# A state-space layer with its feed-forward on one core: the later sequences' first chunks of x turned by VectorE and memory, and the new state one projection tile later

## The reference, cut to what matters

```python
proj = input_states @ in_proj_w.T                 # gate, x, B, C, dt
xBC = silu(depthwise_conv(xBC) + conv_b)          # 4 taps
dt = softplus(dt + dt_bias); cum = cumsum(dt * A) # within a chunk
scores = (C @ B^T) * exp(cum_i - cum_j) * mask * dt_j
y_intra = scores @ x
state   = cdec * state + (dt * dlast * x)^T @ B   # carried over chunks
y_inter = (C * exp(cum)) @ state_before
g = (y_intra + y_inter + D * x) * silu(gate)
x = x + (g * rsqrt(mean(g^2) + eps)) * norm_w @ out_w.T
x = x + ffn(layernorm(x))                         # SwiGLU with low-rank terms
```

## Time and profile before

| | us |
|---|---|
| median of 3 runs | 1725.38 |
| lowest and highest | 1725.22, 1727.03 |
| time of the profiled execution | 1728.03 |
| its span, first to last instruction | 1726.2 |
| mean granted TensorE clock, share of full | 0.997 |

### The profile page before, as it was taken

How to read it: one execution, slowest core, us unless ns; L and a number is a source line. 1 busy time by engine, 2 the same in 40 slices (tenths; PEclk the granted TensorE clock), 3 DMA queues, 4 the chain that set the end, 5 groups by cost and what they waited for, 6 DMA issues and landing times.

```text
span 1726.2 us, 27380 instructions
## 1 busy us (share of the span) xinstructions
PE 1697.8 (98%) x9541; PEld 1406.2 (81%) x9541; DVE 1302.7 (75%) x2202; ACT 1194.5 (69%) x2232; POOL 1228.3 (71%) x1058
## 2 busy tenths in 40 slices
PE   8889999999999999999999999999999999999999
PEld 7768888888888888888888888888888888787887
DVE  8888688968797879778886879687977799663323
ACT  6857777776877777767877777778777777663411
POOL 5567778777787878777878778777877787774510
PEclk9999999999999999999999999999999999999999
DMA  5564636555655455554745565555555573554201
GB/s 185 159 177 132 171 115 207 154 157 159 198 157 146 142 158 190 152 166 133 201 128 170 149 199 160 156 158 176 154 152 151 149 212 114 156 148 135 83 12 49
DMA packets 156617, 261.96 MB, mean 152 GB/s; under 512 B 28097, under 2 KB 57409, under 8 KB 156481
## 3 DMA queue, kind: packets, MB, share of 16 engines
q1 hardware_dynamic: 156480, 260.21, 51.8%
HBM read 230.25 MB, written 29.89 MB: 151 GB/s over the span
## 4 chain that ended last, share of the span: by engine, by line
PE 89%; DVE 5%; POOL 2%; DMA 2%; issue 1%; ACT 1%; SPq 0%; DVEq 0%; POOLq 0%; ACTq 0%
PE bank L1813 18%; PE bank L1815 17%; PE bank L1814 17%; PE bank L1891 7%; PE bank L1942 6%; PE bank L1935 6%; PE bank L1952 6%; PE bank L1906 4%; DVE ow_l L1458 2%; PE bank L2197 1%; PE bank L2196 1%; PE bank L2198 1%; PE bank L1968 1%; DVE bcT L1452 1%; PE bank L1875 1%
## 5 line engine op out<-in xcount | busy, mean ns | idle before, releaser
L763 POOL TENSOR_TENSOR w_l<-w_raw,w_h 128x512 fp32r<-128x512 f32 x288 | 398.0, 1384 | 267.3 <-ACT w_h L967 267.1
L1813 PE MATMUL bank<-x_h,w_h 128*128 128x512 f32 (+1 forms) x1328 | 527.7, 397 | 10.2 <-DVE bcT L1452 5.9
L1815 PE MATMUL bank<-x_h,w_l 128*128 128x512 f32 (+1 forms) x1328 | 519.4, 391 | 0.0
L1814 PE MATMUL bank<-x_l,w_h 128*128 128x512 f32 (+1 forms) x1328 | 518.7, 391 | 0.0
L1020 ACT ACTIVATE decay<-decay,cols 128x128 f32<-128x128 f32 x1024 | 318.3, 390 | 9.8 <-POOL decay L769 8.1
L1452 DVE SCALAR_TENSOR_TENSOR x_ch<-bank,par,x_ch 128x511 f32<-128x511 f32 (+2 forms) x384 | 286.3, 746 | 34.1 <-ACT x_ch L985 25.0
L1813 PEld LDWEIGHTS bank<-x_h,w_h 128*128 128x128 f32 (+1 forms) x1328 | 249.8, 188 | 64.6 <-issue 12.3
L1815 PEld LDWEIGHTS bank<-x_h,w_l 128*128 128x128 f32 (+1 forms) x1328 | 249.5, 188 | 54.2
L1814 PEld LDWEIGHTS bank<-x_l,w_h 128*128 128x128 f32 (+1 forms) x1328 | 250.0, 188 | 50.6
L769 POOL TENSOR_SCALAR_AFFINE_SELECT decay<-decay 128x512 f32<-128x512 f32 x256 | 200.3, 799 | 73.0 <-DMA decay<-cum_scratch 72.0
L1506 DVE TENSOR_TENSOR decay<-decay,bank 128x512 f32<-128x512 f32 x256 | 171.0, 682 | 82.6 <-ACT decay L1020 82.6
(11 more groups left out here) (164 smaller groups left out, 2793.5 us busy)
## 6 DMA issues: line engine op xcount, KB each, us to landing
w_raw<-in_wp SPq DMA_DIRECT2D x288, 256.0 KB, 3.5
decay<-cum_scratch SPq DMA_DIRECT2D x256, 256.0 KB, 4.7
x_rows<-xt_scratch SPq DMA_DIRECT2D x48, 512.0 KB, 3.3
ec<-ecum_scratch SPq DMA_DIRECT2D x96, 256.0 KB, 7.0
ow_raw<-in_ow SPq DMA_DIRECT2D x64, 256.0 KB, 5.4
xt_scratch<-xw_sq SPq DMA_DIRECT2D x128, 128.0 KB, 3.0
w_raw<-in_w SPq DMA_DIRECT2D x48, 256.0 KB, 2.7
xt_scratch<-ec_sq SPq DMA_DIRECT2D x64, 128.0 KB, 2.4
```

The costliest lines, as they stand in the source:

```text
L763: pool.tensor_tensor(w_l[:, s, :], w_raw[:, s, :], w_h[:, s, :].bitcast(F32), ALU.subtract).then_inc(wl_ready, 1)
L1813: pe.matmul(dst, wh, xh, start=(opens and k == 0), stop=False)
L1814: pe.matmul(dst, wh, xl, start=False, stop=False)
L1815: last = pe.matmul(dst, wl, xh, start=False, stop=(k == len(terms) - 1 and not more))
```

## The change

1. `on_pe(K)` is true for K = 0, 1 and 2 alone. Chunks 1 and 2 of the first group now go by TensorE as chunk 0 does, and the first chunks of all later sequences (K = 4, 8, ..., 60) go by DVE and memory.
2. There are four scratch areas and four semaphores in memory, one for each c, where there were two. The turned x of a chunk with c = 0 lies in `gT_sq` (the bytes of `gT_l`), that with c = 2 in `xh_sq` (the bytes of `xw_h`). The fetched rows for c = 0 go to `xw`.
3. In a slot with c = 3, DVE turns the next chunk right behind `add_skip`, ahead of `mean_square` and `gated`; SP stores it, stores the chunk two further, and then waits for the first store to land and fetches it. DVE's `scale_x` stands behind the first quarter's `scores` in place of ahead of `accumulate`. POOL's `gT_low` there waits for the store, since it writes where `gT_sq` lay.
4. In a slot with c = 0 (not K = 0), TensorE computes the first projection tile ahead of `new_state`, the second behind it, and then `match` and `across`. DVE does `mean_square` and `gated` ahead of `add_state`.
5. At the start, DVE's `turn_x(0, 1)` and its store are gone, and POOL's `gT_low` no longer waits for `xdt_ready` where the next chunk goes by TensorE. In the first three chunks `new_state` waits for `xdt_ready`, since it writes the banks that `scale_x` reads.

The diff, cut to its core:

```diff
-            return ec_sq if k % SC == 1 else xw_sq
+            return (gT_sq, ec_sq, xh_sq, xw_sq)[k % SC]
+        def rows_at(k):
+            return xw if k % SC == 0 else x_rows
+        def on_pe(K):
+            return K < SC - 1
+        def moved_no(K):
+            return K - SC + 2
@@ SP, fetch_x
-                sp.wait_ge(x_stored[K % 2], stored_no(K))
-                if some(K - 1):
+                if on_pe(K):
+                    return
+                sp.wait_ge(x_stored[K % SC], stored_no(K))
+                if k % SC > 0:
                     sp.wait_ge(out_done, 2 * (K - 1))
-                sp.dma_start(x_rows[:, :], xt_dram[K % 2]).then_inc(x_fetched, 16)
+                sp.dma_start(rows_at(k)[:, :], xt_dram[K % SC]).then_inc(x_fetched, 16)
@@ SP, body
-                    if c == 1 or first:
+                    if c == 1:
                         store_x(g, k + 2)
                     if c == SC - 1:
+                        store_x(gn, kn)
                         store_x(gn, kn + 2)
+                        fetch_x(gn, kn)
@@ POOL, gT_low
                 pool.wait_ge(gTh_ready, K + 1)
-                if c < SC - 1:
+                if c == SC - 1 and K < GROUPS * CHUNKS - 1:
+                    pool.wait_ge(x_stored[0], stored_no(K + 1))
+                elif K < GROUPS * CHUNKS - 1 and not on_pe(K + 1):
                     pool.wait_ge(xdt_ready, K + 2)
@@ ACT, xw_high
+                if k % SC == 0 and some(K):
+                    act.wait_ge(x_stored[2], stored_no(K + 2))
@@ DVE, body
                     add_skip(g, k)
+                    if c == SC - 1:
+                        turn_x(gn, kn)
                     if first:
                         ...
+                    elif c == 0:
+                        mean_square(*before)
+                        gated(g, k)
+                        add_state(g, k)
                     else:
                         add_state(g, k)
                         mean_square(*before)
                         gated(g, k)
...
+                    if c == SC - 1:
+                        accumulate(*before)
+                        turn_x(gn, kn + 1)
+                        scores(gn, kn, 0)
                     scale_x(gn, kn)
@@ TensorE, body
+                    late_state = c == 0 and not first
+                    if late_state:
+                        projects(tiles[:1])
                     new_state(g, k)
                     if first:
                         projects(tiles[3:4])
-                    if not first:
+                    if late_state:
+                        projects(tiles[1:2])
+                    elif not first:
                         ...
                     if last and c == SC - 1:
                         match(gn, kn)
                         projects(tiles[1:-1])
-                        turn_x(gn, kn)
                     else:
-                        if c == SC - 1:
+                        if on_pe(gn * CHUNKS + kn):
                             turn_x(gn, kn)
                         match(gn, kn)
```

More of the change, by code:

```diff
@@ L180, in build @@
         xdt = sc("xdt", [P, GCH])
+        xh_sq = under("xh_sq", [P, QUADS, CT, SQ])
         xw_h = sc("xw_h", [P, GCH], F32R)
@@ L189, in build @@
         x_rows = under("x_rows", [P, GCH])
+        gT_sq = under("gT_sq", [P, QUADS, CT, SQ])
         gT_l = sc("gT_l", [P, CT, P], F32R)
@@ L334, in build @@
         x_turned = sem("x_turned")
-        x_stored = [sem(f"x_stored{n}") for n in range(2)]
+        x_stored = [sem(f"x_stored{n}") for n in range(SC)]
         x_fetched = sem("x_fetched")
@@ L695, in body @@
                             load_decay(gn, kn, q)
-                    if c == 0:
+                    if c == 0 and some(K):
                         sp.wait_ge(x_stored[1], stored_no(K + 1))
@@ L784, in weigh_x @@
                 if c == 2:
[L785 to L789, removed]
+                    pool.wait_ge(x_stored[SC - 1], stored_no(K + 1))
                 pool.tensor_tensor(per_head(xw[:, :]), per_head(xdt[:, :]), spread(cols[:, b, ELAST, c, :], HDIM),
@@ L1490, in turn_x @@
                 dve.wait_ge(silu_done, conv_no(2 * g + b, CONV_TILES))
-                if c == 1 and some(K - 1):
+                if c == 0:
+                    dve.wait_ge(out_done, 2 * (K - 1))
+                if c == 1:
                     dve.wait_ge(z_scaled, n_across(g, k))
                 if c == 2:
-                    dve.wait_ge(st_done, n_state(g, k - 2) if some(K - 2) else 1)
+                    dve.wait_ge(st_done, n_state(g, k - 2))
                 if c == SC - 1:
@@ L1758, in body @@
                             ow_low(g, j)
+                    if c == SC - 1:
+                        accumulate(*before)
+                        turn_x(gn, kn + 1)
+                        scores(gn, kn, 0)
                     scale_x(gn, kn)
-                    if not first:
+                    if not first and c < SC - 1:
                         accumulate(*before)
-                    if c == SC - 1:
-                        turn_x(gn, kn + 1)
                     if k == 0:
@@ L1771, in body @@
                     taps_of(tiles[1:2])
+                    if k == 0 and not first:
+                        fade(gn, kn)
                     if k > 0:
                         scale_across(gn, kn)
-                        scores(gn, kn, 0)
+                        if c < SC - 1:
+                            scores(gn, kn, 0)
                         scores(gn, kn, 1)
@@ L2161, in body @@
                     if not first:
-                        projects(tiles[1:3])
+                        projects(tiles[2 if c == 0 else 1:3])
                     out_half(g, k, 0)
```

42 lines of the change are left out of this document (19 added, 23 removed).

## The result

| | before | changed |
|---|---|---|
| median, us | 1725.77 (4 runs) | 1801.85 (4 runs) |
| profiled execution, its span | 1728.03, 1726.2 | 1801.73, 1799.9 |
| mean granted clock | 0.997 | 0.979 |

The ratio is 1.043, 95% interval 1.0418 to 1.0443. The forecast was 1750 (1730 to 1775): the sign was right and the place too, the size was not. The spans differ by 73.7 us. Compared by the starts of TensorE's 64 `inside` blocks in both timelines, they fall so: -10.2 up to slot K = 4; +80.0 in the 14 slots K = 4 to 56 that follow a border, 4.8 to 7.0 in each; -0.4 in the 14 slots ahead of those borders; +5.1 in slot K = 59; -0.8 behind. All other slots agree within 0.1.

A forecast was written before the change was run, and what follows sets the result against it. TensorE's list was taken to bound the kernel. Borders +21, last border +2, slots k = 0 +6, start -8 and clock +3 gave +24 on the median 1725.38: 1749.4, rounded to 1750 us, range 1730 to 1775.

The forecast's parts named there:

- What bounds the kernel: Whole kernel: TensorE, busy 1697.8 of 1726.2 us; only its work removed or its waits change the time.
- The chain at the border: Store, fetch, `scale_x`, POOL, ACT, `scores` at 14 borders: TensorE stands 2.1 us in `inside`, net +1.5 each, +21.
- lands 3.3 later: Border chain: the fetch of x, issued at T + 5.1, lands 3.3 us later, at T + 8.4.
- By the Trainium skill: Border DMAs estimated at 2.3 us a store, 3.2 the fetch; each border 0.8 cheaper, still a loss.
- Transposes taken off: TensorE at the borders: 15 turns of 0.63 us go, -9.5; two come at K = 1, 2, +1.3.
- The step on POOL: Border chain: `weigh_x` takes 1.92 us, to T + 11.7; `gT_low` ahead, starting with the landed store, is long done.
- The clock: Behind the stands of 2.1 us at the borders: half clock at 2 of 14, +3 (0 to 24).
- The rival: Same stands, but half clock for 3.4 us behind most borders, 24 in place of 3: about 1771; chance 0.15.
- Slots k = 0: State one tile later: 0.9 us more wait for DVE's taps in each of 7 groups, +6 (3 to 9).
- The start: First chunks: the fetch chain behind TensorE's 6.58 us wait and the half clock go, -8 (-11 to -4).
- The last border: Last group's border: DVE's `norm_apply` behind `scale_x` comes 3.3 us late for TensorE, net +2 (0 to 4).
- SP's list: Rival: SP's wait for the landed store delays the loads behind it, 2 us more a border, 1778; chance 0.05.

The follow-up runs named there:

- e2_state: The kernel before with the new order of the slots c = 0 alone; 1727.99 us, ratio 1.0008.
- e5_delay: The kernel before with mutually waiting ACT copies ahead of the fourth exponentials, a different count at each of 14 borders, new tile placed last; 1775.64 us, ratio 1.0280.
- e12_fetch: The changed kernel with the store of `xh_sq` put behind the fetch of x in place of ahead of it; 1777.99 us, ratio 1.0278.
- e3_xwh: The changed kernel with ACT's `xw_high` behind the last exponentials in slots with c = 3; 1776.9 us, ratio 1.0287.
- e4_delay: The kernel before with 8 to 30 one-column ACT copies ahead of the last exponentials, another number at each of 14 borders; 1746.65 us, ratio 1.0112.
- e6_order: The changed kernel with `xw_high` behind the last exponentials, POOL's sums ahead of `weigh_x` and DVE's four `scores` ahead of `scale_x`, where c = 3; 1781.4 us, ratio 1.0308.

## Why the prediction was wrong

- **What bounds the kernel**: right. Only TensorE's list counted, and all 80 us lie where five lists meet at the border.
- **The chain at the border**: right in every link and order. It was short by 1.85 at its end: 0.4 at the store's landing, 1.5 in the fetch, nothing behind it. The step that failed first is the fetch that "lands 3.3 later": that term took the median of fetches of other slots and measured 4.8 to `scale_x`. "Two other stores are still under way, which may stretch it" had the cause, and was given no number. The stretch of the changed kernel above shows DMA engines 0.92 busy during the fetch; where a fetch of before runs I had not read it. It is 0.72 (366.6 to 369.9, the same columns):

```profile
366.60:369.90 3.30, 3.30 (x40) 2.91 (x37) 2.17 (x8) 2.10 (x4) 3.30 (x3) 1.00 0.72 235
```

  The fourth quarter came 3.3 late in place of 2.1, and with 0.5 to 0.7 more behind it (drains behind ACT's `xw_high`, and the restart) it was 3.8 a border: 54 us where the sum had 29.
- **By the Trainium skill**, "DMA: Bandwidth & Descriptors", the anatomy of one DMA: the estimate from its fixed part and its rate was 3.2 for the fetch. The rows have 4.6 here and 3.8 without the store ahead: the fit has no term for what is queued ahead, which here cost 0.8.
- **Transposes taken off**: the 0.63 at 14 borders was not gained. It was to be 8.8 us and is 0.4, since TensorE now waits for POOL's `gT_l` ahead of `inside` (the row at 364.09: 0.43, and a slower start behind it), which waits for the landed store. The step on POOL named that wait ("starts with the landed store") and looked only at what POOL did next, not at TensorE, which wants `gT_l` at T + 7.6.
- **The clock**: "2 borders of 14: +3" failed; it was 14 of 14 and about 24 us in the tile behind the stand alone (4.58 in the mean, 2.85 for the same order in e2_state), some 2 more where half clock lasted 6.8 us. I had set 2.1 between the rows at 1.53 and 2.48 and taken the cheap side. In this place e5_delay had full clock up to 1.72 and half clock from 1.97, e12_fetch half clock at 12 of 14 stands of 2.08 to 3.07; in e3_xwh, with stands of 1.44 to 2.11 ahead of `square_total`, it came 10 times of 14. A fourth quarter that is 3.3 late shows as 3.0 of idle time in the row, so the forecast's 2.1 would be some 1.8 there (an estimate from these two), between e5_delay's 1.72 and 1.97: the longer chain carried the stands past what had left full clock there. The rival had this mechanism, 1771 with a chance of 0.15; the longer stands (+24) and the turns given back (+8) carry it to 1803, less what k = 0 and the start fell short.
- **Slots k = 0**: +6 was forecast, about 1 came. The step carried the later start on to the taps and gave back only the 0.51 at `accumulate`; it left out that `scale_x` would be 1.1 shorter where it now stands (e2_state). **The start**: -8, measured -10.2, in the range. **The last border**: the forecast had DVE's `norm_apply` behind `scale_x` 3.3 late; the row has TensorE waiting 4.0 for it, half clock lay behind that too (0.50 from 1541.6 to 1548.3), and the sum is +4.3 for +2. **SP's list**: no load of weights was late.

Sum of the misses from +24 to +73.7: stands +24, clock +21 to +23, turns given back +8, last border +2, k = 0 -5, start -2; that leaves at most 2 us unplaced.

The likeliest case and the worst rival were not independent: a longer chain made the stand longer, and the longer stand made the clock's fall likelier. The range treated them apart and so ended 27 us short. It was also narrower than its own terms: their upper bounds add up to +69, about 1794, where the recorded text has 1768 without a working.

## What to carry to other kernels

Where a transfer enters a chain, follow each list behind every engine that waits for it to its end, not only to the next reader: here `scores`, the sum of squares and the drains stood behind one another, and each removal only showed the next. Price a DMA by what is queued ahead of it at that moment, not by its median elsewhere. And a stand of the bound engine has two prices here, with and without half clock behind it: if rows of like length show both, take the dear one.

## What the runs showed that I had not expected

**A few bytes' shift.** In e4_delay a tile of 128 bytes a partition stood ahead of most others; in the kernel's order `x_h`, `x_l` and `acc` come before it, the tiles of weights behind it. Products of a tile then started 0.233 apart (2.80 / 12) and no longer 0.227, a tile took 2.80 where it took 2.72 (343.84 - 341.12 in the timeline of before), and the whole kernel some 15 us more:

```profile
342.63 0.40 PE L1817 MATMUL bank<-x_h,w_h 128*128 128x512 f32 x1
342.87 0.39 PE L1818 MATMUL bank<-x_l,w_h 128*128 128x512 f32 x1
343.09 0.40 PE L1819 MATMUL bank<-x_h,w_l 128*128 128x512 f32 x1
343.33 0.39 PE L1817 MATMUL bank<-x_h,w_h 128*128 128x512 f32 x1
...
345.43 1.08 PE L1956 MATMUL bank<-ow_h,gT_h 128*128 128x512 f32 x4
```

In e5_delay the new tile, one column wide, stood last, and products were 0.227 apart again. That the place is the cause is the plain reading; which tile's place matters was not tried.

**The clock's step is not sharp.** In e3_xwh eight stands of 2.10 or 2.11 were followed by half clock and three of 2.10 or 2.11 by full clock; those of 1.44 and 1.83 were followed by half clock, that of 1.57 by full. In e6_order three of 2.42 to 2.79 kept full clock and eleven of 2.6 to 2.8 did not; e12_fetch adds the two of 2.12 and 2.44 above. What decides between equal stands stays open.
